# Cross-attention scores in four equal chunks, one per PSUM bank, in a fused decoder layer

## The chip, the cores and the metric

The kernel runs on one core of one Trainium2 chip. The metric is the device time of one execution in microseconds, median of the runs shown. The profile is of one execution on the same core.

## What is computed

One pre-norm decoder layer in fp32 on x of 2048 x 256: page-causal self-attention with rotary embedding (16 heads of 16), then cross-attention to 1601 context rows with one head of width 1024, then a feed-forward layer with quantized activations and ternary weights. The part that the change touches is the cross-attention:

```python
Q = q @ Wq.T + bq
K = k @ Wk.T + bk
V = v @ Wv.T + bv
e = jnp.einsum('bsd,btd->bst', Q, K) / jnp.sqrt(jnp.float32(d_k))
e = jnp.where(mask == 0, MASK_FILL, e)
a = jax.nn.softmax(e, axis=-1)
y = jnp.einsum('bst,btd->bsd', a, V)
return y @ Wo.T + bo
```

Here q is the normed x (2048 x 256), k and v are the context (1601 x 256), and the mask is int32, 2048 x 1601.

## The kernel before

Three stages run one after the other, each a block in which every engine has its own instruction stream and waits on semaphores.

`self_attention` works through 4 blocks of 512 queries. `fold` adds the attention's output to x, norms it, and folds the projections: Wq with Wk into `w_qk` (256 x 256), Wv with Wo into `w_vo`, so that keys and values of width 1024 are never made. It splits the transposed context into a high and a low fp32r piece (`ctx_parts`) and computes the first four of the seven value jobs (a job is two tiles of 128 context rows, V_EARLY = 4 at line 58). The other three stand at the head of the next stage (line 1586).

`cross` is the stage of the change. It walks over 16 tiles of 128 queries. `pairs` writes out tiles 0 and 1, loops over tiles 2 to 13 two at a time, and writes out tiles 14 and 15. The slot h is the tile's parity: the score rows `e[:, h, :]` and the mask rows `mask[:, h, :]` have two slots. For each tile:

- TensorE, `score` (line 1489 on): scores of a tile as products of split fp32r pieces. For each chunk of columns there are six products (two halves of the 256 inner values, three pairs of pieces). The chunks are 512, 512, 512 and 66 columns wide; they fill banks 0 to 3 without gaps, so that the 1601 scores lie in one run. Part 0 is the first two chunks, 12 products; part 1 the other two, 12 products.
- GpSimd, `fill` (line 1295): writes the row's fill value to `e` ahead of the scores. `lower_query` (line 1287) makes the low piece of the query two tiles ahead.
- VectorE, `take`: copies the scores over the fill where the mask is set (line 1323, a predicated copy out of PSUM), takes the maximum (line 1325) and scales it (line 1327).
- ScalarE, `exponential` (line 1452): the exponential in place with the row sum.
- TensorE, `turn_probs` (line 1547): 13 transposes of the exponentials into three banks in four groups, 4 + 4 + 4 + 1. ScalarE copies each group to the high piece (line 1462), VectorE subtracts to get the low piece (line 1378).
- TensorE, value products (line 1577): 13 pairs of 512 and 256 columns into `y_bank`. VectorE scales and adds the result to x (lines 1397 and 1400) and takes the statistics (1404, 1409); GpSimd and VectorE norm the row.

The order is written out by hand. In the body of tile i TensorE does: part 0 of the scores of tile i+1, then (once tile i's exponential is done) 12 transposes of tile i, then part 1 of the scores of tile i+1, the thirteenth transpose, and the 26 value products:

```python
def body(i, h, last):
    if not last:
        score(i + 1, 1 - h, 0)
    ...
    pe.wait_ge(exp_done, i + 1)
    ...
    for n in range(3):
        turn_probs(n)
    if not last:
        score(i + 1, 1 - h, 1)
    pe.wait_ge(p_low, i * NCH + 1)
    turn_probs(3)
```

VectorE in the same body: four subtractions of tile i, `take` of tile i+1, then norm work of earlier tiles and the output of tile i. GpSimd fills `e` for tile i+2 once all 13 transposes of tile i are done. Behind tile 15 come the feed-forward products (lines 1523 and 1534).

Of the kernel before, what the change touches and what calls it, by code (L numbers as in the profile page):

```python
# [18 lines left out]
I32 = mybir.dt.int32  # L19
U32 = mybir.dt.uint32  # L20
ALU = mybir.AluOpType
ACT = mybir.ActivationFunctionType
AX_X = mybir.AxisListType.X
ReduceOp = bass.bass_isa.ReduceOp

P = 128
# [5 lines left out]
BLK = 512  # L32
# [18 lines left out]
S2 = 1601  # L51
S2_TILES = -(-S2 // P)
S2_TAIL = S2 - (S2_TILES - 1) * P
S2_EVEN = S2 + S2 % 2
DH = 1024
HC = DH // P
X_SCALE = float(DH) ** -0.5
# [13 lines left out]
def banks(psum, first, n=1):  # L71
    return psum[:, first * BLK:(first + n) * BLK]
# [717 lines left out]
def fold(nc, ctx, io, keep, psum):  # L790
# [7 lines left out]
    def sem(name):  # L798
        return ctx.enter_context(nc.semaphore(name))
# [5 lines left out]
    qc_parts, qc_high, qc_low = keep["qc_parts"], keep["qc_high"], keep["qc_low"]  # L805
# [58 lines left out]
    ctx_pad = sem("ctx_pad")  # L864
# [9 lines left out]
    with nc.Block() as block:  # L874

        @block.sync
        def _(sp):
            sp.dma_start(b_o[:, :], bass.AP(io["bo"].tensor, 0, [[0, P], [1, E]])).then_inc(b_o_loaded, 16)
            sp.dma_start(ffn_w[:, :, :], io["ffn_w"].rearrange("(c p) e -> p c e", p=P)).then_inc(ffn_w_loaded, 16)
            masks = io["mask"].rearrange("(t p) s -> t p s", p=P)  # L880
            for name in ("gamma", "beta"):
                sp.dma_start(keep[name + "_row"][:, :], bass.AP(io[name].tensor, 0, [[0, P], [1, E]]))\
                    .then_inc(keep["rows_loaded"], 16)
            for h in range(2):
                sp.dma_start(keep["mask"][:, h, :], masks[h]).then_inc(keep["mask_loaded"][h], 16)

        @block.gpsimd
        def _(pool):
            nc.gpsimd.memset(eps[:, :], LN_EPS).then_inc(set_done, 1)  # L889
            nc.gpsimd.memset(minus_half[:, :], -0.5).then_inc(set_done, 1)  # L890
            nc.gpsimd.memset(ones[:, :], 1.0).then_inc(ones_set, 1)
            for part in ctx_parts:
                nc.gpsimd.memset(part[:, :, S2:S2_EVEN].bitcast(F32), 0.0).then_inc(ctx_pad, 1)
            pool.wait_ge(set_done, 2)

            def norm(tb):
                pool.wait_ge(mv_done, tb * TPB + TPB)
                nc.gpsimd.tensor_tensor(var[:, :], mv[:, :, 1], eps[:, :], ALU.add).then_inc(var_done, 1)
                pool.wait_ge(var_done, tb + 1)
                nc.gpsimd.tensor_tensor(rstd[:, :], var[:, :], minus_half[:, :], ALU.pow).then_inc(rstd_done, 1)  # L900

                pool.wait_ge(row_done, 2)
                pool.wait_ge(xn_ready, tb * TPB + TPB)
                tiles = x[:, bass.ds(tb * TPB, TPB), :]
                bias = row_b[:, :].unsqueeze(1).to_broadcast([P, TPB, E])
                nc.gpsimd.tensor_tensor(tiles, tiles, bias, ALU.add).then_inc(bias_added, 1)

            with pool.Fori(0, NB) as tb:
                norm(tb)
            for h in range(2):  # L910
                pool.wait_ge(qc_high, h + 1)
                nc.gpsimd.tensor_tensor(qc_parts[1][:, h, :, :], x2_t[:, :, 0, h * P:(h + 1) * P],
                                        qc_parts[0][:, h, :, :].bitcast(F32), ALU.subtract).then_inc(qc_low, 1)
# [225 lines left out]
def cross(nc, ctx, io, keep, psum):  # L1139
    def sb(name, shape, dt=F32):  # L1140
        return ctx.enter_context(nc.sbuf_tensor(name, shape, dt))

    def sem(name):
        return ctx.enter_context(nc.semaphore(name))
# [7 lines left out]
    x3_low = [flat[tb // 3][:, tb % 3 * EC * BLK:(tb % 3 + 1) * EC * BLK].rearrange("p (c t) -> p c t", c=EC)  # L1152
              for tb in range(NB)]
    mask, w_vo = keep["mask"], keep["w_vo"]
    zeros = sb("zeros_s2", [P, S2])
    qc_parts, qc_high, qc_low = keep["qc_parts"], keep["qc_high"], keep["qc_low"]
    e = sb("e", [P, 2, S2])
    neg = sb("neg", [P, 2])
    esum = sb("esum", [P, 2])
    rsum = sb("rsum_x", [P, 2])  # L1160
# [6 lines left out]
    scale = sb("scale3", [P, 1])  # L1167
# [9 lines left out]

    CHUNKS = [(c * TPB, min(TPB, S2_TILES - c * TPB)) for c in range(-(-S2_TILES // TPB))]
    NCH = len(CHUNKS)
    e_bank = psum[:, 0:S2_EVEN]  # L1180
    t_bank = [banks(psum, n) for n in (4, 5, 7)]
    y_bank = banks(psum, 6)
    v_bank = {4: banks(psum, 6), 5: banks(psum, 7), 6: banks(psum, 5)}
# [5 lines left out]
    mask_loaded, rows_loaded = keep["mask_loaded"], keep["rows_loaded"]  # L1189
# [4 lines left out]
    e_taken = sem("e_taken")  # L1194
    max_done = sem("max_done")
# [45 lines left out]
    with nc.Block() as block:  # L1241

        @block.sync
        def _(sp):
            masks = io["mask"].rearrange("(t p) s -> t p s", p=P)
            with sp.Fori(0, PAIRS - 1) as k:
                for h in range(2):

                    sp.wait_ge(e_taken, 2 * k + h + 1)
                    sp.dma_start(mask[:, h, :], masks[2 * k + (h + 2)]).then_inc(mask_loaded[h], 16)  # L1250

            out = io["out"].rearrange("(u t p) e -> u p t e", p=P, t=2)
            for u in range(UNITS):
                sp.wait_ge(out_added, u + 1)
                sp.dma_start(out[u], x[:, 2 * u:2 * u + 2, :]).then_inc(out_sent, 16)
            sp.wait_ge(out_sent, 16 * UNITS)

        @block.gpsimd
        def _(pool):
# [30 lines left out]
            def fill(i, h):  # L1290
                if isinstance(i, int):
                    value = row_fill[:, i:i + 1]
                else:
                    value = row_fill[:, bass.ds(i, 1)]
                nc.gpsimd.tensor_tensor(e[:, h, :], zeros[:, :], value.to_broadcast([P, S2]),  # L1295
                                        ALU.add).then_inc(filled, 1)

            def body(i, h, last):
# [16 lines left out]
        def _(dve):  # L1315
            def take(i, h):

                dve.wait_ge(mask_loaded[h], (i - h) * 8 + 16)
                dve.wait_ge(filled, i + 1)
                dve.wait_ge(e_ready, i + 1)  # L1320

                dve.sem_inc(waits_met, 1)
                nc.vector.copy_predicated(e[:, h, :], mask[:, h, :], e_bank[:, 0:S2]).then_inc(e_taken, 1)  # L1323
                dve.wait_ge(e_taken, i + 1)
                nc.vector.tensor_reduce(neg[:, h:h + 1], e[:, h, :], axis=AX_X, op=ALU.max).then_inc(max_done, 1)  # L1325
                dve.wait_ge(max_done, 2 * i + 1)
                nc.vector.tensor_scalar(neg[:, h:h + 1], neg[:, h:h + 1], -X_SCALE, None,  # L1327
                                        ALU.mult).then_inc(max_done, 1)
# [114 lines left out]
        def _(act):  # L1443
# [5 lines left out]

            def exponential(i, h):  # L1450
                act.wait_ge(max_done, 2 * i + 2)
                nc.scalar.activation(e[:, h, :], e[:, h, :], ACT.Exp, scale=X_SCALE, bias=neg[:, h:h + 1],  # L1452
                                     accum_out=esum[:, h:h + 1]).then_inc(exp_done, 1)

            def body(i, h, last):
# [29 lines left out]
            for tb in range(NB):  # L1485
                nc.scalar.activation(over[:, tb, :, :], x3_t[:, tb, :, :], ACT.Relu,
                                     bias=bound[:, 1:2]).then_inc(over_done, 1)

        @block.tensor
        def _(pe):  # L1490
            def score(i, h, part):

                if part == 0:
                    pe.wait_ge(e_taken, i)
                    pe.wait_ge(qc_low, i + 1)
                starts = list(range(0, S2, BLK))
                for c0 in (starts[:2], starts[2:])[part]:
                    c1 = min(c0 + BLK, S2_EVEN)
                    products = [(k, *pieces) for k in range(EC) for pieces in ((0, 0), (0, 1), (1, 0))]
                    for k, left, right in products:  # L1500
                        last = nc.tensor.matmul(e_bank[:, c0:c1], qc_parts[left][:, h, k, :],  # L1501
                                                ctx_parts[right][:, k, c0:c1], start=(k, left, right) == products[0],
                                                stop=(k, left, right) == products[-1])
                if part == 1:
                    last.then_inc(e_ready, 1)
# [77 lines left out]
            for n in range(V_EARLY, len(V_JOBS)):  # L1583
                for m, j in enumerate(V_JOBS[n]):
                    for k in range(EC):
                        last = nc.tensor.matmul(v_bank[n][0:keys_of(j), m * E:(m + 1) * E],  # L1586
                                                ctx_t[:, k, j * P:j * P + keys_of(j)], w_vo[:, k, :],
                                                start=k == 0, stop=k == EC - 1)
# [23 lines left out]
def build(nc, io):  # L1612
    with ExitStack() as outer:
        def sb(name, shape, dt=F32):
            return outer.enter_context(nc.sbuf_tensor(name, shape, dt))

        psum = outer.enter_context(nc.psum_tensor("psum", [P, 8 * BLK], F32))
        keep = {"x": sb("x_sb", [P, TILES, E]), "ident": sb("ident", [P, P])}
        with ExitStack() as own:
            def sbo(name, shape, dt=F32):  # L1620
                return own.enter_context(nc.sbuf_tensor(name, shape, dt))
# [18 lines left out]
            keep["w_qk"] = sbo("w_qk", [P, EC, E])  # L1640
            keep["w_vo"] = sbo("w_vo", [P, EC, E])
            keep["ones"] = sbo("ones", [P, P])
            keep["mask"] = sbo("mask", [P, 2, S2], I32)
            keep["gamma_row"] = sbo("gamma_row", [P, E])
            keep["beta_row"] = sbo("beta_row", [P, E])
            keep["mask_loaded"] = [own.enter_context(nc.semaphore(f"mask_loaded{n}")) for n in range(2)]
# [75 lines left out]
```

## Time and profile before

| | |
|---|---|
| median of 3 runs | 813.98 us (813.0 to 814.86) |
| the profiled execution | 815.49 us |
| its span, first to last instruction | 813.6 us |
| mean granted TensorE clock | 0.962 |
| busy: TensorE products, weight loads | 753.8 us, 394.8 us |
| busy: VectorE, ScalarE, GpSimd | 620.8 us, 427.2 us, 150.2 us |
| cross-attention | from 608 us on |

A busy time is the union of an engine's instructions. TensorE's products overlap their successors, and weight loads overlap products, so the price of one product is the distance from one start to the next and not its own duration. The chain of waits lists, from the last instruction backwards, what released each step, and is shown in order of time.

### The profile page before, as it was taken

What the parts mean: (1) busy time and instruction counts of PE and PEld (TensorE: products, weight loads), DVE (VectorE), ACT (ScalarE), POOL (GpSimd) and SP (SyncE); (2) the same over time, 40 slices, a digit from 0 to 9 for tenths busy, and PEclk for the clock granted to TensorE, in tenths of its full rate; (3) what the DMA queues carried; (4) which work ended last, traced back from release to release, by engine and by line L of the source; (5) the groups of instructions that cost most, each with busy time, mean ns of one, the idle gap of its engine ahead of it and who ended that gap; (6) DMA issues with size and microseconds to landing.
All of it is one profiled execution on the core that took longest, in us unless ns stands there. A gap on an engine that the chain in (4) does not pass through costs nothing. (4 is left out here: it accounts for less than half of the span.)

```text
span 813.6 us, 12188 instructions
## 1 busy us (share of the span) xinstructions
PE 753.8 (93%) x4329; PEld 394.8 (49%) x4329; DVE 620.8 (76%) x1107; ACT 427.2 (53%) x879; POOL 150.2 (18%) x170
## 2 busy tenths in 40 slices
PE   7874897999999999999999997989999999999997
PEld 5431232333223333223333331268658888888886
DVE  4899687888998889999888762037736777787885
ACT  1453263676667776666777875932133333333353
POOL 2555000000000000000000000003314555555520
PEclk9997698899999999999999998999999999999999
DMA  7598341020000000000180000030002122222103
GB/s 211 166 254 257 54 118 40 1 67 27 27 2 2 0 2 1 1 1 1 48 254 2 1 1 2 1 114 1 0 1 78 56 70 81 81 81 81 40 1 104
DMA packets 27152, 47.32 MB, mean 58 GB/s; under 512 B 6112, under 2 KB 23008, under 8 KB 26336
## 3 DMA queue, kind: packets, MB, share of 16 engines
q1 hardware_dynamic: 25184, 43.94, 18.0%
q10 hardware_dynamic: 1920, 2.75, 1.2%
q8 instruction: 29, 0.48, 0.3%
q14 instruction: 19, 0.16, 0.1%
HBM read 38.16 MB, written 8.39 MB: 57 GB/s over the span
## 5 line engine op out<-in xcount | busy, mean ns | idle before, releaser
L495 DVE TENSOR_REDUCE part_max<-psum 128x1 f32<-128x512 f32 (+3 forms) x560 | 341.3, 668 | 54.6 <-PE psum L681 49.5
L600 ACT ACTIVATE probs<-psum 128x512 f32<-128x512 f32 (+3 forms) x640 | 293.7, 539 | 154.9 <-PE psum L706 153.9
L681 PE MATMUL psum<-k_stack,q_stack 96*128 96x512 bf16 (+4 forms) x640 | 214.8, 364 | 18.8 <-DVE psum L481 11.5
L706 PE MATMUL psum<-q_stack,k_stack 98*128 98x512 bf16 (+4 forms) x640 | 202.2, 357 | 13.4 <-DMA q_stack<-shift 11.6
L718 PE MATMUL psum<-probs,v_all 128*17 128x512 f32 (+3 forms) x1280 | 149.1, 538 | 0.3
L681 PEld LDWEIGHTS psum<-k_stack,q_stack 96*128 96x128 bf16 (+1 forms) x640 | 60.1, 99 | 171.6 <-DVE part_max L495 120.9
L706 PEld LDWEIGHTS psum<-q_stack,k_stack 98*128 98x128 bf16 (+1 forms) x640 | 60.9, 99 | 94.4 <-ACT probs L600 39.0
L889 POOL MEMSET eps<- 128x4 f32 x1 | 0.1, 102 | 459.0 <-POOLq L282 459.0
L1501 PE MATMUL psum<-ctx_part,qc_part 128*128 128x512 f32 (+1 forms) x384 | 82.9, 366 | 1.8 <-PEq L874 1.8
L1577 PE MATMUL psum<-v_parts,p_part 128*128 128x512 f32 (+3 forms) x416 | 77.3, 342 | 0.0
L1501 PEld LDWEIGHTS psum<-ctx_part,qc_part 128*128 128x128 f32 x384 | 66.3, 189 | 14.5 <-issue 2.6
L1577 PEld LDWEIGHTS psum<-v_parts,p_part 128*128 128x128 f32 (+1 forms) x416 | 64.0, 188 | 8.7
L1452 ACT ACTIVATE e<-e,neg 128x1601 f32<-128x1601 f32 x16 | 26.2, 1636 | 68.0 <-DVE neg L1327 63.4
L1378 DVE TENSOR_TENSOR p_part<-psum,p_part 128x512 fp32r<-128x512 f32 x64 | 34.7, 585 | 25.7 <-ACT p_part L1462 25.7
L1295 POOL TENSOR_TENSOR e<-zeros_s,row_fill 128x1601 f32<-128x1601 f32 x16 | 45.6, 2853 | 35.8 <-PE psum L1547 35.7
L1462 ACT ACTIVATE p_part<-psum 128x512 fp32r<-128x512 f32 x64 | 29.6, 518 | 37.4 <-PE psum L1547 37.4
L718 PEld LDWEIGHTS psum<-probs,v_all 128*17 128x17 f32 x1280 | 21.4, 95 | 49.4 <-ACT probs L600 36.7
L1323 DVE COPY_PREDICATED e<-mask,psum 128x1601 f32<-128x1601 int32 x16 | 33.1, 2069 | 9.8 <-PE psum L1501 9.1
L518 DVE RECIPROCAL rsum<-psum 128x16 f32<-128x16 f32 x16 | 4.1, 253 | 38.1 <-PE psum L692 37.6
L1325 DVE TENSOR_REDUCE neg<-e 128x1 f32<-128x1601 f32 x16 | 29.1, 1821 | 0.6
L1547 PE MATMUL psum<-ident,e 128*128 128x128 f32 (+1 forms) x208 | 28.5, 275 | 1.0 <-DVE p_part L1378 0.7
L1045 PE MATMUL psum<-q_stack 128*128 128x256 f32 (+2 forms) x128 | 26.3, 357 | 0.0
(145 smaller groups left out, 689.2 us busy)
## 6 DMA issues: line engine op xcount, KB each, us to landing
mask<-in_mask SPq DMA_DIRECT2D x16, 800.5 KB, 4.3
pieces<-k_stack SPq DMA_DIRECT2D x24, 256.0 KB, 4.7
q_stack<-pieces SPq DMA_DIRECT2D x24, 256.0 KB, 4.3
k_stack<-pieces SPq DMA_DIRECT2D x24, 256.0 KB, 4.7
x_sb<-in_x SPq DMA_DIRECT2D x4, 512.0 KB, 9.2
out<-x_sb SPq DMA_DIRECT2D x8, 256.0 KB, 2.2
q_stack<-in_ctxT SPq DMA_DIRECT2D x1, 1601.0 KB, 11.0
probs<-in_cos ACTq DMA_DIRECT2D x4, 256.0 KB
```

What stands on the lines that cost most here:

```text
L495: nc.vector.tensor_reduce(part_max[:, h:h + m, r, c:c + 1], src, axis=AX_X, op=ALU.max).then_inc(m_read, 1)
L600: nc.scalar.activation(probs[:, s % 2, h, col:BLK], s_bank[h][:, col:BLK], ACT.Exp, scale=ATTN_SCALE).then_inc(exp_done, 1)
L681: last = nc.tensor.matmul(out, q_stack[b][0:rows, g * G + h, r * P:(r + 1) * P], k_stack[c][0:rows, g * G + h, 0:keys], start=True, stop=True)
L706: nc.tensor.matmul(s_bank[h][:, col:BLK], k_stack[s // TPB][0:rows, g * G + h, (s % TPB) * P:(s % TPB + 1) * P], q_stack[b][0:rows, g * G ...
L718: last = nc.tensor.matmul(o_bank[32 * h:32 * h + VW, col:BLK], v_all[:, s, g * G + h, :], probs[:, s % 2, h, col:BLK], start=s == 0, stop= ...
L1295: nc.gpsimd.tensor_tensor(e[:, h, :], zeros[:, :], value.to_broadcast([P, S2]), ALU.add).then_inc(filled, 1)
L1323: nc.vector.copy_predicated(e[:, h, :], mask[:, h, :], e_bank[:, 0:S2]).then_inc(e_taken, 1)
L1325: nc.vector.tensor_reduce(neg[:, h:h + 1], e[:, h, :], axis=AX_X, op=ALU.max).then_inc(max_done, 1)
L1378: nc.vector.tensor_tensor(p_parts[1][0:rows, j:j + m, :].rearrange("p j q -> p (j q)"), t_bank[n % 3][0:rows, 0:m * P], p_parts[0][0:rows, ...
L1462: nc.scalar.activation(p_parts[0][0:rows, j:j + m, :].rearrange("p j q -> p (j q)"), t_bank[n % 3][0:rows, 0:m * P], ACT.Copy).then_inc(p_ ...
L1501: last = nc.tensor.matmul(e_bank[:, c0:c1], qc_parts[left][:, h, k, :], ctx_parts[right][:, k, c0:c1], start=(k, left, right) == products[ ...
L1577: mm = nc.tensor.matmul(cols, p_parts[part][0:keys, j, :], values, start=j == 0 and part == 0, stop=end and part == 0)
```

## The change

The scores of a tile are computed in four chunks of 402 columns (1608 in all), each at the start of a bank of its own (0 to 3). Part 0 is chunks 0 and 1, part 1 chunks 2 and 3. The context pieces are padded with zeros from 1601 to 1608 columns. `e`, the mask and the zeros are 1608 wide. The predicated copy reads `[128, 4, 402]` out of the four banks; the pad of the mask is set to 0 once, in the folding stage. The maximum and the exponential take the first 1601 elements, as before. The value jobs stay where they were.

```diff
-S2_EVEN = S2 + S2 % 2
+QUARTER = 402
+S2_EVEN = 4 * QUARTER
...
-                sp.dma_start(keep["mask"][:, h, :], masks[h]).then_inc(keep["mask_loaded"][h], 16)
+                sp.dma_start(keep["mask"][:, h, 0:S2], masks[h]).then_inc(keep["mask_loaded"][h], 16)
...
             for part in ctx_parts:
                 nc.gpsimd.memset(part[:, :, S2:S2_EVEN].bitcast(F32), 0.0).then_inc(ctx_pad, 1)
+            nc.gpsimd.memset(keep["mask"][:, :, S2:S2_EVEN], 0).then_inc(ctx_pad, 1)
...
-    zeros = sb("zeros_s2", [P, S2])
+    zeros = sb("zeros_s2", [P, S2_EVEN])
...
-    e = sb("e", [P, 2, S2])
+    e = sb("e", [P, 2, S2_EVEN])
...
-    e_bank = psum[:, 0:S2_EVEN]
+    e_bank = banks(psum, 0, 4).rearrange("p (n s) -> p n s", n=4)
...
-                nc.gpsimd.tensor_tensor(e[:, h, :], zeros[:, :], value.to_broadcast([P, S2]),
+                nc.gpsimd.tensor_tensor(e[:, h, :], zeros[:, :], value.to_broadcast([P, S2_EVEN]),
...
-                nc.vector.copy_predicated(e[:, h, :], mask[:, h, :], e_bank[:, 0:S2]).then_inc(e_taken, 1)
+                quarters = [row[:, h, :].rearrange("p (n s) -> p n s", n=4) for row in (e, mask)]
+                nc.vector.copy_predicated(*quarters, e_bank[:, :, 0:QUARTER]).then_inc(e_taken, 1)
...
-                nc.vector.tensor_reduce(neg[:, h:h + 1], e[:, h, :], axis=AX_X, op=ALU.max).then_inc(max_done, 1)
+                nc.vector.tensor_reduce(neg[:, h:h + 1], e[:, h, 0:S2], axis=AX_X, op=ALU.max).then_inc(max_done, 1)
...
-                nc.scalar.activation(e[:, h, :], e[:, h, :], ACT.Exp, scale=X_SCALE, bias=neg[:, h:h + 1],
+                nc.scalar.activation(e[:, h, 0:S2], e[:, h, 0:S2], ACT.Exp, scale=X_SCALE, bias=neg[:, h:h + 1],
...
-                starts = list(range(0, S2, BLK))
-                for c0 in (starts[:2], starts[2:])[part]:
-                    c1 = min(c0 + BLK, S2_EVEN)
+                for n in (2 * part, 2 * part + 1):
+                    c0, c1 = n * QUARTER, (n + 1) * QUARTER
...
-                        last = nc.tensor.matmul(e_bank[:, c0:c1], qc_parts[left][:, h, k, :],
+                        last = nc.tensor.matmul(e_bank[:, n, 0:QUARTER], qc_parts[left][:, h, k, :],
...
-            keep["mask"] = sbo("mask", [P, 2, S2], I32)
+            keep["mask"] = sbo("mask", [P, 2, S2_EVEN], I32)
```

On TensorE, in the loop body of the cross-attention (a tile's scores at L1501, its transposes at L1547, the value products at L1577), the order before is:

```order
L1501 MATMUL psum<-ctx_part,qc_part 128x512 [waits qc_low]
L1501 MATMUL psum<-ctx_part,qc_part 128x512 x11
L1547 MATMUL psum<-ident,e 128x128 [waits exp_done3]
L1547 MATMUL psum<-ident,e 128x128 x11
L1501 MATMUL psum<-ctx_part,qc_part 128x512 x6
L1501 MATMUL psum<-ctx_part,qc_part 128x66 x6
L1564 ISA
L1547 MATMUL psum<-ident,e 65x128 [waits p_low]
L1577 MATMUL psum<-v_parts,p_part 128x512 [waits p_low,x_added3]
```

And now, where the same lines are L1503, L1549 and L1579:

```order
L1503 MATMUL psum<-ctx_part,qc_part 128x402 [waits qc_low]
L1503 MATMUL psum<-ctx_part,qc_part 128x402 x11
L1549 MATMUL psum<-ident,e 128x128 [waits exp_done3]
L1549 MATMUL psum<-ident,e 128x128 x11
L1503 MATMUL psum<-ctx_part,qc_part 128x402 x12
L1566 ISA
L1549 MATMUL psum<-ident,e 65x128 [waits p_low]
L1579 MATMUL psum<-v_parts,p_part 128x512 [waits p_low,x_added3]
```

The number of products and their waits stay; the six narrow ones at the end of the second group are gone, and all 24 have one width.

## Rows read from the trace of the kernel before

**Rows 1.** The page, busy time: us, share of the span, instructions.

```profile
PE 753.8 (93%) x4329; PEld 394.8 (49%) x4329; DVE 620.8 (76%) x1107; ACT 427.2 (53%) x879; POOL 150.2 (18%) x170
```

**Rows 2.** Chain of waits, cross-attention, in order of time: start us, us, step.

```profile
608.66 5.01 PE psum L1501 x24
...
620.86 1.31 PE psum L1547 x12
...
661.32 2.79 PE psum L1501 x12
664.10 1.31 PE psum L1547 x12
665.41 1.99 PE psum L1501 x12
667.54 4.59 PE psum L1577 x26
672.13 2.79 PE psum L1501 x12
...
773.55 1.99 PE psum L1501 x12
776.40 2.07 DVE e L1323
...
790.39 4.67 PE psum L1523 x40
...
802.91 5.27 PE psum L1534 x48
```

**Rows 3.** Timeline, tiles 4 and 5: start us, us, instruction, idle before it.

```profile
659.72 0.74 POOL L1287 TENSOR_TENSOR qc_part<-x_t,qc_part 128x256 fp32r<-128x256 f32 x1
660.93 2.74 PEld L1501 LDWEIGHTS psum<-ctx_part,qc_part 128*128 128x128 f32 x12
...
663.11 0.18 ACT L1452 ACTIVATION_READ_ACCUMULATOR e<-e,neg 128x1 f32 x1
...
663.94 1.47 PE L1547 MATMUL psum<-ident,e 128*128 128x128 f32 x12
664.34 0.18 DVE L1409 BATCH_NORM_AGGREGATE mv<-stats 128x2 f32<-128x6 f32 x1 [0.24 <-DVE stats L1404]
...
665.21 1.89 DVE L1378 TENSOR_TENSOR p_part<-psum,p_part 128x512 fp32r<-128x512 f32 x3 [0.69 <-ACT p_part L1462]
...
667.88 0.29 DVE L1378 TENSOR_TENSOR p_part<-psum,p_part 65x128 fp32r<-65x128 f32 x1 [0.79 <-ACT p_part L1462]
668.23 2.06 DVE L1323 COPY_PREDICATED e<-mask,psum 128x1601 f32<-128x1601 int32 x1
```

**Rows 4.** Timeline, the last tile, where TensorE waits for the exponential.

```profile
782.14 0.18 ACT L1452 ACTIVATION_READ_ACCUMULATOR e<-e,neg 128x1 f32 x1
...
782.38 1.53 PE L1547 MATMUL psum<-ident,e 128*128 128x128 f32 x12 [0.37 <-ACT e L1452]
```

**Rows 5.** Timeline, the first tile.

```profile
612.90 2.85 POOL L1295 TENSOR_TENSOR e<-zeros_s,row_fill 128x1601 f32<-128x1601 f32 x1
...
619.91 0.18 ACT L1452 ACTIVATION_READ_ACCUMULATOR e<-e,neg 128x1 f32 x1
```

**Rows 6.** Groups by line and form, 490 to 760 us: busy us, mean ns, idle.

```profile
L1501 PEld LDWEIGHTS psum<-ctx_part,qc_part 128*128 128x128 f32 x344 | 59.5, 189 | 13.3 <-issue 2.6
...
L1323 DVE COPY_PREDICATED e<-mask,psum 128x1601 f32<-128x1601 int32 x14 | 29.0, 2069 | 9.7 <-PE psum L1501 9.1
...
L1325 DVE TENSOR_REDUCE neg<-e 128x1 f32<-128x1601 f32 x14 | 25.5, 1821 | 0.5
L1378 DVE TENSOR_TENSOR p_part<-psum,p_part 128x512 fp32r<-128x512 f32 x39 | 24.5, 684 | 11.9 <-ACT p_part L1462 11.9
...
L1378 DVE TENSOR_TENSOR p_part<-psum,p_part 65x128 fp32r<-65x128 f32 x13 | 3.7, 287 | 10.2 <-ACT p_part L1462 10.2
```

**Rows 7.** Stretches: us, busy per engine (PE, PEld, DVE, ACT, POOL), PEclk, DMA share, GB/s.

```profile
613.00:785.00 172.00, 170.95 (x1002) 148.35 (x1001) 134.46 (x215) 62.72 (x112) 87.13 (x102) 1.00 0.20 67
```

More of the change, by code:

```diff
@@ L1249, in _ @@
                     sp.wait_ge(e_taken, 2 * k + h + 1)
-                    sp.dma_start(mask[:, h, :], masks[2 * k + (h + 2)]).then_inc(mask_loaded[h], 16)
+                    sp.dma_start(mask[:, h, 0:S2], masks[2 * k + (h + 2)]).then_inc(mask_loaded[h], 16)
             out = io["out"].rearrange("(u t p) e -> u p t e", p=P, t=2)
```

## Prediction

> **What bounds the kernel now.** I read the page first. TensorE is busy for 93% of the span, VectorE for 76%, the others for much less [rows 1], so TensorE may be the bound, but a busy share is a mean over three stages, and the change touches one: the cross-attention, from 608 us on. The chain of waits in order of time settles it for that stage. Between the first score products and tile 14 it holds TensorE groups and nothing else, with the same four lengths in each tile: 12 products of scores 2.79 us, 12 transposes of the exponentials 1.31, the other 12 score products 1.99, the value products 4.59 [rows 2]. With 0.13 for the thirteenth transpose this makes the period: 672.13 - 661.32 = 10.81 us, 14 times alike from tile 0 to tile 14 (622.17 to 773.55). Only behind tile 14, where no scores are left to compute, does the chain leave TensorE, for VectorE's predicated copy at 776.40 and what follows it: maximum, exponential, transposes.
>
> So each tile is a ring of two loops. The engine loop is what TensorE must do in a tile. The softmax loop runs through the same transposes: transposes, second score group, last transpose, ScalarE's copy and VectorE's subtraction of that transpose, predicated copy, maximum, exponential, and the next tile's transposes. The timeline of tile 4 tells how far the second is behind the first [rows 3]: the exponential's accumulator is read out at 663.11 + 0.18 = 663.29, and the 12 transposes end at 663.94 + 1.47 = 665.41, that is 2.12 later. Where TensorE really waits for the exponential, in the last tile, the same stretch is 782.32 to 783.91, 1.59 us [rows 4]. The softmax loop has **0.53 us of slack**; it would close at 10.28 us.
>
> **The change, part by part.**
>
> *The products.* Before, a tile takes 18 products of 512 columns and 6 of 66; now 24 of 402. A 512-wide one costs 2.79 / 12 = 0.232 us [rows 2]. The narrow ones: second group and last transpose together are 667.54 - 665.41 = 2.13; less a transpose (1.31 / 12 = 0.11) and six wide ones (1.39) leaves 0.63, or 0.104 each, nearly as much as a 128-column transpose. A 66-column product is paid like one of some 230 columns, and that is what the change removes. The trace has no 402-column product. Its price by the wide ones is 402/512 x 0.232 = 0.182; by the last stage's 256-column products of the same type, 4.67 / 40 = 0.117 [rows 2], it is 402/256 x 0.117 = 0.183. I take 0.183. The lower end is the bf16 products of 256 columns, 5.27 / 48 = 0.110, which give 0.172; the upper end is one whole weight load, 0.189 [rows 6], in case each product waited for its own load (the 256-wide ones do not), say 0.188.
> Then the scores cost 24 x 0.183 = 4.39 where they cost 2.79 + 2.13 - 0.11 = 4.81: **the engine loop falls by 0.41, to 10.40 us**. The granted clock is 1.00 from 613 to 785 us [rows 7], so all of these are prices at 2.4 GHz.
> The Trainium skill, "TensorE: Matmul & The Clock Gate", section "Back-to-back issue gap", gives N/2.4 + 2.5 ns for an isolated product. That is 216 ns for 512 columns where the trace has 232, and it would be 170 ns for 402. By it the sum below would be about 8 us and not 5.5, an estimate from that page's figure. I go by the trace, since it is 7% above that rule at 512 and at 256 columns alike.
>
> *Where they stand.* The 12 of the first group get shorter, 2.79 to 2.20, but the second group, which lies on the softmax loop, had the cheap narrow ones and gets longer: 12 x 0.183 + 0.11 = 2.31 instead of 2.13, **+0.18 on the softmax loop**. Its end is not waited for by the predicated copy itself: that starts at 668.23, behind the last subtraction (667.88 + 0.29), which hangs on the last transpose [rows 3]. So the whole shift of the transpose is passed on.
>
> *The predicated copy* reads four runs of 402 instead of one of 1601: 7 elements more, 2069 ns / 1601 x 7 = 0.01 us [rows 6]. That the three gaps between runs cost nothing I assume (the other value is a rival, below). Maximum and exponential still take 1601 elements. The fill on GpSimd grows by 7 elements (0.01 us); the query piece behind it ends at 660.46, and the next scores' weights are loaded at 660.93 [rows 3], and both hang on the last transpose, so that cover of 0.47 stays. The extra memset and the wider pads stand at the start of the folding stage, where GpSimd idles; the mask's DMA keeps its size and gets a tile to land. I cost these at nothing.
>
> *Sum per tile.* The softmax loop closes at 10.81 - 0.53 + 0.18 + 0.01 = 10.47 us, the engine loop at 10.40. The first is now the later: TensorE is predicted to wait for the exponential in each tile, and **0.34 of the 0.41 us arrive**. VectorE must also be free when the transposes come 0.53 sooner behind the exponential: it ends its statistics at 664.34 + 0.18 = 664.52 and starts the subtractions at 665.21 [rows 3], so 0.16 is left. It just holds.
> *Total.* The end of tile 0's transposes: the 24 products at the head get 4.81 - 4.39 = 0.42 shorter; the chain through mask and exponential moves with them, since the first fill is done when the second starts, at 612.90, and the shortened scores end at about 613.67 - 0.42 = 613.25 [rows 2, 5]; then its slack is used up, which is 0.49: the accumulator's 619.91 + 0.18 to the transposes' 620.86 + 1.31 is 2.08, less 1.59 [rows 2, 4, 5]. That is -0.91. Fourteen periods: -4.76. Tile 14 to 15 was bound by the softmax loop already and gets +0.19. Together **-5.5 us**. The profiled execution took 815.49 us (span 813.6), so it would take 810.0; against the median of 813.98 that is **808.5 us**. At 0.172 per product the same sum gives -1.17 - 14 x 0.48 + 0.05 = -7.8, at 0.188 it gives -0.79 - 14 x 0.28 + 0.25 = -4.5. The slack is read against the last tile, whose code is written out and not in a loop; should 0.16 of it not be there in the loop (my allowance), it is about -3.
>
> **The rivals.**
> *A, the engine stays the bound.* The softmax loop would have to be 0.07 shorter than I read it. For it: the two loops end up that close. Against: the second group's lengthening follows from the prices. Time: -1.0 - 14 x 0.41 + 0.2 = -6.5, 807.5 us.
> *B, a 402-column product costs 0.172 or less*, so that the second group hardly grows: -7.8, 806.2 us. Against: both fp32r rows give 0.182 to 0.183. (The rule of the Trainium skill's page on TensorE, section "Back-to-back issue gap", leads to this case.)
> *C, slower: the gathered PSUM read.* If each of the four runs pays a start of its own, the predicated copy, which is on the loop that now binds, gets longer. A VectorE instruction's fixed part is, from the subtraction's 684 ns at 512 and 287 at 128 elements [rows 6], 287 - 128 x 1.034 = 0.155 us; three more make 0.46. The softmax loop is then 10.93 (+0.12), tile 0 moves by -0.45, tile 15 by +0.65: +1.9, 815.9 us. It decides from 5.5 / 16 = 0.34 us more per copy on. For it: this copy takes 2069 ns where the maximum over as many elements takes 1821 [rows 6], so something in it already costs 0.25 us. Against: nothing shows it to be the bank changes.
>
> **How the numbers follow.** My forecast has a chance of 0.70, A 0.07, B 0.08, C 0.08; 0.07 is left for a part of the gain lost in a place that I don't see. This kernel's measurement can tell about 0.2% (1.6 us) from no change. Forecast, A and B lie beyond it, with some of the rest: faster 0.88, same 0.05, slower 0.07. The forecast's own range, by the two prices, is 806.2 to 809.5; with the case of the smaller slack (811) and the scatter of the runs (0.9 to each side) I give 805.8 to 811.6; C lies outside.
>
> **What would show it.** Right: score products 0.183 apart in both groups; a period near 10.47; the chain of waits passing through the predicated copy, the maximum and the exponential in each tile instead of TensorE alone; a wait of TensorE for the exponential of about 0.1 us per tile; the copy at 2.08. Wrong: a period of 10.40 and a chain of TensorE alone (A), products 0.172 or less apart (B), a copy of over 2.3 us (C), or VectorE's first subtraction starting late behind its statistics.

## The result and the profile after

The changed kernel took 805.03 us (median of 4 runs, 804.85 to 806.43), the kernel before 813.6 us (4 runs) beside it. The ratio is 0.9895, with a 95% interval of 0.988 to 0.9909. The forecast of 808.5 had the direction right and the size too small, and the time lies 0.8 us below the range. The profiled execution of the changed kernel took 805.07 us, its span 803.3 us.

The groups of the page, changed kernel (columns as in [rows 6]):

```profile
L1503 PE MATMUL psum<-ctx_part,qc_part 128*128 128x402 f32 x384 | 77.2, 350 | 1.8 <-PEq L875 1.8
...
L1503 PEld LDWEIGHTS psum<-ctx_part,qc_part 128*128 128x128 f32 x384 | 69.6, 189 | 3.3 <-issue 2.6
...
L1326 DVE COPY_PREDICATED e<-mask,psum 128x1608 f32<-128x1608 int32 x16 | 32.0, 2000 | 9.4 <-PE psum L1503 8.7
```

All 384 score products have 402 columns. The predicated copy takes 2000 ns where it took 2069 [rows 6], with 7 elements more.

The chain of waits of the changed kernel in order of time, to be held against [rows 2]:

```profile
606.16 4.66 PE psum L1503 x24
...
617.35 1.39 PE psum L1549 x12
618.75 2.20 PE psum L1503 x12
...
627.86 1.36 PE psum L1549 x12
...
638.32 1.37 PE psum L1549 x12
...
657.01 2.21 PE psum L1503 x12
659.22 1.31 PE psum L1549 x12
660.53 2.21 PE psum L1503 x12
662.74 0.11 PE psum L1549
662.84 4.59 PE psum L1579 x26
667.44 2.21 PE psum L1503 x12
...
764.70 2.20 PE psum L1503 x12
...
781.62 4.68 PE psum L1525 x40
...
789.49 3.08 PE psum L1525 x24
```

A group of 12 score products is 2.21 us, 0.184 each, in both places. The period in tile 4 is 667.44 - 657.01 = 10.43 us, and from tile 0 (617.35 + 1.39 = 618.74) to tile 14 (764.70) it is 145.96 / 14 = 10.425 on average. The chain still holds TensorE alone up to tile 14, as in [rows 2].

The average hides two kinds of period. The first two, which end with the transposes of tiles 1 and 2, take 10.475 us each (618.74 to 639.69), and the groups of transposes of tiles 0 to 2 are longer than the 1.31 us of transposes that wait for nothing. The other twelve take 10.42 (639.69 to 764.70), with 1.31 in each. Before, all fourteen were 10.81. Experiment 3 comes back to this.

The timeline says that this is a near tie. Changed kernel, tile 4 (compare [rows 3]):

```profile
658.74 0.18 ACT L1455 ACTIVATION_READ_ACCUMULATOR e<-e,neg 128x1 f32 x1
...
658.98 1.31 PEld L1549 LDWEIGHTS psum<-ident,e 128*128 128x128 f32 x12
659.05 1.48 PE L1549 MATMUL psum<-ident,e 128*128 128x128 f32 x12
659.30 0.43 DVE L1407 BATCH_NORM_STATS2 stats<-x_sb 128x6 f32 x1
...
662.57 0.27 PE L1549 MATMUL psum<-ident,e 128*65 128x128 f32 x1
...
663.19 0.29 DVE L1381 TENSOR_TENSOR p_part<-psum,p_part 65x128 fp32r<-65x128 f32 x1 [0.81 <-ACT p_part L1465]
663.53 2.01 DVE L1326 COPY_PREDICATED e<-mask,psum 128x1608 f32<-128x1608 int32 x1
```

The transposes' first weights are loaded 0.06 us behind the read-out of the accumulator (658.92 to 658.98), so the exponential does hold them now. They end at 660.53, 1.61 us behind the read-out; the closed loop of the last tile takes 1.59 [rows 4], and before there were 2.12 [rows 3]. The slack is used up. But the last product of the scores still runs, until 659.22 (656.85 + 2.37), when the transposes start at 659.05, and their group in the chain is the shortest, 1.31, so next to nothing is lost by it in this tile.

Where the two profiles differ, stretch by stretch, from the first and last rows of each:

| stretch | before | after | difference | predicted |
|---|---|---|---|---|
| start to the first score product | 608.66 | 606.16 | -2.50 | 0 |
| to the end of tile 0's transposes | 13.51 | 12.58 | -0.93 | -0.91 |
| 14 periods | 151.38 | 145.96 | -5.42 | -4.76 |
| tile 14's to tile 15's transposes | 10.36 | 10.46 | +0.10 | +0.19 |
| behind them to the end | 29.7 | 28.1 | -1.6 | 0 |

The stage of the change gives 6.25 us. The other 4.1 us stand in code that is the same in both kernels, but for one small memset and the wider pads. In both places TensorE's clock differs. Granted clock and busy times of the kernel before, around its last 24 high and low products (columns as in [rows 7]):

```profile
795.00:798.20 3.20, 1.61 (x12) 1.20 (x11) 2.10 (x7) 2.00 (x4) 0.00 (x0) 1.00 0.00 0
798.20:801.70 3.50, 3.43 (x16) 3.43 (x17) 2.04 (x4) 3.41 (x5) 0.00 (x0) 0.52 0.00 0
```

And of the changed kernel in the same place of the program:

```profile
786.30:789.40 3.10, 1.56 (x12) 1.20 (x11) 2.02 (x7) 1.98 (x4) 0.00 (x0) 1.00 0.00 0
...
790.00:793.00 3.00, 3.00 (x28) 2.90 (x28) 1.61 (x3) 3.00 (x4) 0.00 (x0) 1.00 0.02 5
```

TensorE was half idle ahead of both (busy for 1.61 of 3.20 us and 1.56 of 3.10). In the one the clock then stood at 0.52, nearly all of it at the lower level of 1.2 GHz, and the 24 products took 4.64 us; in the other it stayed at 2.4 GHz and they took 3.08. Near the start of the program, between 14 and 20 us, the clock differs too (kernel before, then changed):

```profile
14.00:20.00 6.00, 3.34 (x4) 1.50 (x5) 2.08 (x10) 2.37 (x3) 1.33 (x2) 0.72 0.54 160
```

```profile
14.00:20.00 6.00, 4.37 (x11) 2.01 (x12) 2.54 (x10) 1.47 (x3) 1.33 (x2) 1.00 0.54 154
```

Not all of the 2.50 us of the first row is the clock's. The timelines of the two show that TensorE starts the first eight products of line 639 (in the changed kernel 640) at 16.66 and at 15.63 us, 1.03 apart. They wait for a copy by ScalarE, which is still issuing the loading transfers until 14.10 and 13.07. The eight products then take 5.37 us at the low clock and 3.67 at the full one.

### The profile page after: what moved, and what is told of

The parts are those of the page before. It is cut to its first block and busy times, and to the rows that moved or that the text cites. A ratio compares the mean times of both kernels' runs of the same rounds, so it can differ in the third digit from the quotient of the medians.

```text
span 803.3 us, 12189 instructions
## 1 busy us (share of the span) xinstructions
PE 745.3 (93%) x4329; PEld 397.5 (49%) x4329; DVE 619.4 (77%) x1107; ACT 427.0 (53%) x879; POOL 150.2 (19%) x171
## 5 line engine op out<-in xcount | busy, mean ns | idle before, releaser
L1503 PE MATMUL psum<-ctx_part,qc_part 128*128 128x402 f32 x384 | 77.2, 350 | 1.8 <-PEq L875 1.8
L1579 PE MATMUL psum<-v_parts,p_part 128*128 128x512 f32 (+3 forms) x416 | 77.3, 342 | 0.0
L1503 PEld LDWEIGHTS psum<-ctx_part,qc_part 128*128 128x128 f32 x384 | 69.6, 189 | 3.3 <-issue 2.6
L1579 PEld LDWEIGHTS psum<-v_parts,p_part 128*128 128x128 f32 (+1 forms) x416 | 63.8, 188 | 9.5
L1297 POOL TENSOR_TENSOR e<-zeros_s,row_fill 128x1608 f32<-128x1608 f32 x16 | 45.8, 2866 | 30.9 <-PE psum L1549 30.9
L1465 ACT ACTIVATE p_part<-psum 128x512 fp32r<-128x512 f32 x64 | 29.6, 517 | 32.6 <-PE psum L1549 32.6
L1326 DVE COPY_PREDICATED e<-mask,psum 128x1608 f32<-128x1608 int32 x16 | 32.0, 2000 | 9.4 <-PE psum L1503 8.7
L1549 PE MATMUL psum<-ident,e 128*128 128x128 f32 (+1 forms) x208 | 28.2, 274 | 1.0 <-DVE p_part L1381 0.7
```

Source lines behind the costliest of these rows:

```text
L1326: nc.vector.copy_predicated(*quarters, e_bank[:, :, 0:QUARTER]).then_inc(e_taken, 1)
L1465: nc.scalar.activation(p_parts[0][0:rows, j:j + m, :].rearrange("p j q -> p (j q)"), t_bank[n % 3][0:rows, 0:m * P], ACT.Copy).then_inc(p_ ...
L1503: last = nc.tensor.matmul(e_bank[:, n, 0:QUARTER], qc_parts[left][:, h, k, :], ctx_parts[right][:, k, c0:c1], start=(k, left, right) == pr ...
L1549: last_t = nc.tensor.transpose(t_bank[n % 3][0:keys, (j - j0) * P:(j - j0 + 1) * P], e[:, h, j * P:j * P + keys], ident[:, :])
L1579: mm = nc.tensor.matmul(cols, p_parts[part][0:keys, j, :], values, start=j == 0 and part == 0, stop=end and part == 0)
```

## Experiments

Two things had to be found out: which of the two loops binds before and after, and whether the head and the tail belong to the change.

**1. Is the softmax loop really 10.28 us before, and closed after?** The same small load was put on it in both kernels: a second copy of the first 402 elements.

```diff
+                nc.vector.copy_predicated(e[:, h, 0:402], mask[:, h, 0:402], e_bank[:, 0:402]).then_inc(copied, 1)
+                dve.wait_ge(copied, i + 1)
...
                 nc.vector.copy_predicated(e[:, h, :], mask[:, h, :], e_bank[:, 0:S2]).then_inc(e_taken, 1)
```

Expected of the kernel before with it:

> The kernel before with a second predicated copy of the first 402 elements put ahead of the whole one (same values, about 0.65 us more on the softmax loop with its wait). Theory of the prediction (0.53 us of slack in the softmax loop before): the period grows by only 0.1 to 0.2, from 10.81 to 10.9 or 11.0, and the time by 2 to 4 us. Rival (no slack, or VectorE bound by its own work): the period grows by the whole 0.65, the time by 10 us.

Expected of the changed kernel with it (the copy there is of the first run of 402):

> The changed kernel with the same extra copy of 402 elements. If the softmax loop touches the engine loop after the change, the whole 0.65 us arrives: period 10.42 to about 11.05, time 805 to about 815 us. If it had slack left, less arrives, by the slack.

Measured: the kernel before went to 817.13 us, ratio 1.004 (1.0025 to 1.0054), and its period from 10.813 to 11.076 (mean of 14), so 0.26 of it arrived. The changed kernel went to 819.34 us, ratio to the kernel before 1.0074 (1.005 to 1.0097), its period from 10.425 to 11.192, so 0.77 arrived. The load itself was larger than the 0.65 expected, so both periods lie above what was expected of them (10.9 to 11.0, and 11.05), and the changed kernel's time lies 4 us above the 815. The chain of waits of the changed kernel with the extra copy shows what the prediction had wanted to see without it:

```profile
658.50 0.63 DVE e L1327
...
659.27 2.03 DVE e L1330
661.32 1.83 DVE neg L1332
...
665.14 1.53 PE psum L1553 x12
666.67 2.20 PE psum L1507 x12
```

The extra copy takes 0.62 us in both kernels, so the softmax loop had 0.5 us more slack before. Over the twelve later periods alone the two are at 11.04 and 11.15. With the softmax loop of the changed kernel at 10.38 there (experiment 3), the load costs 11.15 - 10.38 = 0.77, and the loop of the kernel before is 11.04 - 0.77 = 10.27, where the prediction read 10.28 from one tile's timeline.

**2. Out of the way, and deeper in.** One line sets how many chunks of scores lie on the softmax loop.

```diff
-                for n in (2 * part, 2 * part + 1):
+                for n in ((0, 1, 2), (3,))[part]:
```

> The changed kernel with three of the four 402-column chunks in part 0 (ahead of the transposes) and one in part 1 (behind them). TensorE's work per tile is the same; the softmax loop gets 6 products, 6 x 0.184 = 1.10 us, shorter. Theory 1 (the changed kernel is bound by TensorE's own loop, 10.42 us, with the softmax loop only touching it): the period stays 10.40 to 10.43, the exponential's read-out lies a microsecond ahead of the transposes, time within 0.3% of the changed kernel (805 us). Theory 2 (the changed kernel is still bound by the softmax loop): the period falls to the engine loop of the prediction, 10.36 to 10.40, and the time by 0.3 to 1 us more.

Measured: 806.75 us (6 runs), ratio to the kernel before 0.9918 (0.9899 to 0.9937); period 10.413. This is theory 1, in the period and in the time (0.2% above 805). The read-out now lies well ahead of the transposes, as expected:

```profile
658.64 0.18 ACT L1455 ACTIVATION_READ_ACCUMULATOR e<-e,neg 128x1 f32 x1
660.05 1.47 PE L1549 MATMUL psum<-ident,e 128*128 128x128 f32 x12
```

TensorE's own loop is thus 10.41 us, the same in all periods, the first two included. The changed kernel's twelve later periods, 10.42, are within 0.01 of it, and its first two, 10.475, lie 0.06 above. The other direction, `((0,), (1, 2, 3))[part]`:

> The changed kernel with one chunk of scores ahead of the transposes and three behind them, so six more products, 1.10 us, lie on the softmax loop. As that loop touches TensorE's own, the period should grow by the whole 1.10, from 10.42 to 11.5, the time by about 14 x 1.10 = 15 us less what the head gains. If products behind the transposes were not on the path, the period would stay at 10.42.

Measured, in a single run: 822.74 us, period 11.482, so 1.06 of the 1.10 us arrived, as expected. What stands behind the transposes is on the path once the slack is gone, and the two loops are within 0.04 us of each other.

**3. Which one binds?** Shifting the tiles after `zeros_s2` by 32 bytes makes the value products a little cheaper (experiment 5), on TensorE's loop only.

```diff
+    spacer = sb("spacer", [P, 8])
     e = sb("e", [P, 2, S2_EVEN])
```

> The changed kernel with 32 unused bytes ahead of e, so that e and the transposed exponentials start 32 bytes further on. That made the value products 4.53 us per tile instead of 4.59 in the kernel before, on TensorE's loop alone; it should leave the softmax loop as it is. If the changed kernel is bound by TensorE's loop, its period falls by about 0.05, to 10.37; if by the softmax loop (the prediction's view), it stays within 0.02 of 10.42, with the wait after the read-out 0.05 as before. Time: within 0.1% of the changed kernel, or 0.7 us less.

> The same 32 bytes in the kernel with three chunks ahead of the transposes, where the softmax loop has 1 us of slack. Only TensorE's loop can bind here, so the period should fall by the 0.05 of the value products, from 10.41 to 10.36, and the time by about 0.8 us below the changed kernel's: the fastest of the family, if the address does what it did before.

Measured: the first 806.69 us (4 runs), ratio 0.9916 (0.9891 to 0.9941), period 10.394; the second 805.56 us (4 runs), ratio 0.9897 (0.9874 to 0.992), period 10.341. The chains of the first and the second:

```profile
667.16 2.21 PE psum L1504 x12
669.37 1.34 PE psum L1550 x12
670.72 2.21 PE psum L1504 x12
672.92 0.11 PE psum L1550
673.03 4.51 PE psum L1580 x26
```

```profile
669.35 3.30 PE psum L1504 x18
672.65 1.31 PE psum L1550 x12
673.96 1.10 PE psum L1504 x6
675.06 0.11 PE psum L1550
675.17 4.51 PE psum L1580 x26
```

With the softmax loop out of the way, TensorE's loop falls by the whole 0.07, to 10.34. With it in place the fall stops earlier, and the transposes' group shows the wait, 1.34 where it is 1.31: the twelve later periods are 10.38 (the 10.394 is the mean with the first two). So there the softmax loop of the changed kernel is 10.38 us and TensorE's is 10.41: **in twelve of fourteen periods the change is bound by TensorE's loop, by 0.03 us**. The expectation for a softmax bound, within 0.02 of 10.42, was missed by 0.01 and that for a TensorE bound, 10.37, by 0.02, because each loop takes over in the middle.

The first two periods are another matter. They are 10.47 to 10.48 in the changed kernel, in both of its repeats, with the shift and with `odd_rows` (experiment 4), and 10.41 only in `split31`, where the softmax loop is out of the way. There the softmax loop binds, at 10.475. The timelines show why it is longer: in tiles 1 and 2 of both kernels the exponential starts 0.24 to 0.25 us behind the start of the scaling of the maximum (line 1330, changed kernel: 636.14 to 636.39 in tile 2), from tile 3 to 14 it is 0.18 to 0.19 (657.02 to 657.20 in tile 4). In the kernel before, the slack in tiles 1 and 2 was accordingly 0.45 and not 0.53: the read-out ends at 641.75 and the transposes at 643.79 in tile 2, 2.04 apart. These exponentials stand in the bodies that are written out, the faster ones in the loop; what makes the difference was not tested.

**4. Why is the softmax loop 10.38 and not 10.47?** The copy got 0.07 shorter. Two suspects were the reading of four runs and the row start. The kernel before with both `e` and the mask 1608 wide, all else as it was:

> The kernel before with e and the mask 1608 wide, but products, banks and the copy of one run of 1601 as before. It tells what made the predicated copy 2.00 us and not 2.07: the row start (slot 1 then starts on a multiple of 32 bytes), or the reading of four runs of 402 out of four banks. Row start: the copy takes about 2.00 here too. Runs: it stays at 2.07. The period stays 10.81 in both cases, the time 811 to 816 us.

The changed kernel with rows of 1609:

> The changed kernel with the rows of e and mask 1609 wide instead of 1608, so that the second slot starts at an odd multiple of 4 bytes; nothing else differs. If the row layout made the predicated copy 2.00 us, the copy goes back to about 2.07, at least in one slot, and as the softmax loop touches the engine loop, the period grows by 0.03 to 0.08 from 10.42, toward the 10.47 of the prediction. If not, the copy stays at 2.00 and the period at 10.42.

Measured: `pad_only` 813.85 us, ratio 0.9996 (0.9982 to 1.001), period 10.813; `odd_rows` 808.43 us (4 runs), ratio 0.9919 (0.9893 to 0.9945), period 10.404. The copies:

```profile
L1324 DVE COPY_PREDICATED e<-mask,psum 128x1601 f32<-128x1601 int32 x16 | 31.9, 1995 | 9.8 <-PE psum L1502 9.1
```

```profile
L1327 DVE COPY_PREDICATED e<-mask,psum 128x1608 f32<-128x1608 int32 x16 | 31.9, 1993 | 9.4 <-PE psum L1504 8.7
```

The copy is fast with one run, and fast with odd rows: reading four runs costs nothing, and the start of the second row is not it. If the row layout had done it, the odd rows would have put the copy back to 2.07, and they don't. Their period is 0.02 below the 10.42 expected for that case; the value products take 4.56 us there and not 4.59 (more on them at the end). `pad_only` also shows that a faster copy alone is worth nothing before the change, where that loop had slack.

**5. The address.** The kernel before with 32 bytes ahead of `e`, and with rows of 1608 in `e` alone:

> The kernel before with 32 unused bytes per partition ahead of e, so that e starts 32 bytes further on; rows stay 1601 wide. The copy took 2.07 us before, 2.00 with rows of 1608, 1608 in the change and 1609. If the start address of e decides it, the copy takes 2.00 here; if the row pitch of e or the mask decides it, it stays at 2.07. Period 10.81 either way.

> The kernel before with rows of 1608 in e alone; e starts at the same address, the mask keeps its pitch of 1601. If the pitch of e decides it, the copy takes 2.00; if the start address or the mask's pitch does, it stays at 2.07.

Measured, in a single run each: 810.52 and 811.32 us, period 10.767 in both, a thing not expected. With the shift the copy takes 1998 ns on average, as the start address would have it. With the wide rows of `e` neither expectation holds alone, it depends on the slot. Two successive tiles of that kernel's timeline, slot 1 and slot 0:

```profile
644.71 2.01 DVE L1323 COPY_PREDICATED e<-mask,psum 128x1601 f32<-128x1601 int32 x1
...
655.49 2.08 DVE L1323 COPY_PREDICATED e<-mask,psum 128x1601 f32<-128x1601 int32 x1
```

By the addresses of the built programs, `e` and the mask lie 70656 bytes apart (a multiple of 256) in both slots of the kernel before and in slot 0 of `e_rows`, and these are the slow copies. The fast ones have 70684 bytes (slot 1 of `e_rows`), 70688 (`pad_only`, `shift_e`), 70752 (changed) and 70784 (`odd_rows` and the two shifted kernels of experiment 3). So it is not the pitch; where the two tensors lie with respect to each other fits all cases, but nothing was tried that tells it from other rules on addresses.

**6. Head and tail.** The same two programs again.

> The changed kernel once more, beside the kernel before. The stage of the change is 6.3 us shorter in the two profiles (first scores to the last tile's transposes), the medians are 8.6 us apart. In the profiles seen so far the stretch ahead of the first scores takes 606.3 or 608.6 us and the stretch behind the last transposes 28.1 or 29.7 us, by whether TensorE's clock stood at its lower level in it, in kernels of both kinds. Theory 1 (these two are chance, the change is worth 6.3 us): with more runs the medians come to 6 to 7.5 us apart. Theory 2 (the change also makes the low stretches rarer): they stay 8 to 9 us apart.

> The kernel before, profiled again. Theory 1: head 606 or 608.6 us, tail 28.1 or 29.7 us, in some combination, and the stage itself as in the first profile (period 10.81). Theory 2: head or tail long again, as in its first profile.

> The changed kernel a third time. Theory 1 (worth 6.3 us in its stage, the rest chance of the head and tail): median 806 to 808.5 us, the distance to the kernel before 6 to 7.5 us. Theory 2: 805 us, 8 to 9 us apart.

Measured: the changed kernel 807.0 us (6 runs; ratio 0.991, 0.989 to 0.9929) and 806.06 us (6 runs; 0.9914, 0.9891 to 0.9936), the kernel before 813.74 us (12 runs; 0.9996, 0.9979 to 1.0013). The last 24 products of the changed kernel in `a_again`:

```profile
789.85 4.58 PE psum L1525 x24
```

So this happens to the changed kernel too. The kernel before, in `b_again`, has both a late first score product (607.80) and the slow 24 products (4.63) once more, as theory 2 wanted it, and its stage and period are those of the first profile. The medians are 7.2 us apart in `a_again`, which is theory 1, and 7.9 in `a_third`, between the two theories, though its 806.06 lies in the range of theory 1.

Over all profiles of this study, six of kernels with the old chunks and nine with the new ones, the first score product starts at 607.4 and 607.5 us on average (606.0 to 608.7 and 606.1 to 610.4), and the tail is long (29.6 to 29.7 and not 28.1 to 28.2) in two of six and four of nine. The head is late with a low clock between 14 and 20 us, in three of six and five of nine, and at 606.0 to 606.9 in all the others. Nothing in these profiles ties head or tail to the chunks. All 16 runs of the changed kernel have a mean of 806.3 us and a median of 806.3, the 74 of the kernel before 813.8 and 814.0: 7.5 us, with a standard deviation of 1.2 and 1.4 us, so about 0.7 to either side. Without the first four runs it is 7.2. The first comparison had drawn the changed kernel's lucky end. Theory 1 had said 6 to 7.5, and theory 2 8 to 9. The 1 us between 7.2 or 7.5 and the 6.25 of the stage I cannot place. No stretch of the profiles shows it, and it is a little more than the 0.7 allows for, so it stays open.

## Why the prediction was right or wrong

- *The products.* 0.183 us predicted, 0.184 measured (2.21 / 12). Right. The 256-column products behind that price lie outside [rows 7], but the clock was 1.00 from 789 to 795 us as well. The formula for an isolated product in the Trainium skill, "TensorE: Matmul & The Clock Gate", section "Back-to-back issue gap", N/2.4 + 2.5 ns, makes it 170 ns; the trace has 8% more, about as at 512 columns.
- *TensorE's loop.* 10.40 predicted, 10.41 measured where it stands alone (`split31`). Right.
- *Slack before, 0.53, and the softmax loop at 10.28.* Confirmed for the loop's tiles: a load that cost 0.77 after cost 0.26 before. The slack was read in tile 4; in tiles 1 and 2 it is 0.45 (experiment 3), which the prediction did not look at. The +0.18 of the second group was right too: from the end of the 12 transposes to the start of the predicated copy it was 668.23 - 665.41 = 2.82 us and is now 663.53 - 660.53 = 3.00.
- *Tile 0.* -0.91 predicted, -0.93 measured.
- *"7 elements more, 0.01 us" for the predicated copy*: **this step failed.** Its price moved by -0.07, not by +0.01, and it is the term that decided between the two loops: in the twelve later periods the softmax loop is 10.38 and not 10.47, TensorE's at 10.41 binds, and the mean period is 10.425. Rival A is what happened there, and the 0.07 by which its softmax loop had to be shorter is about what the copy gave (0.39 of a saving of 0.40 arrived, and not 0.34). The rival had 0.07 of the chance. The term is worth 14 x 0.045 + 0.09 = 0.7 us. I had treated a copy's price as a function of its length alone. In the first two periods TensorE does wait for the exponential and the period is the forecast's 10.47, but by luck: the copy is 0.07 shorter there too, and the slack was 0.08 smaller than read.
- *The total.* Stage: -6.25, predicted -5.5. Rival C was wrong: four runs read as fast as one. VectorE was not late where it counts: in every second tile its first subtraction waits 0.31 to 0.33 us for ScalarE's first copy, in the others it starts right behind the statistics (670.52 + 0.18, then 670.75 in tile 5), so the predicted 0.16 is used up there; but the first three subtractions end at 672.64, a microsecond before the fourth starts at 673.61.
- *The range, and head and tail at nothing*: **this step failed too, and it is the larger part.** Of the 3.5 us between 808.5 and 805.03 the stage has 0.75 (6.25 less 5.5); the other 2.7 lie in stages that the change leaves alone, with the 1 us that stays open. I took the scatter from three runs, 0.9 us to either side, and gave even less of it: 806.2 - 0.9 is 805.3, where I wrote 805.8. Over 74 runs the kernel before lies between 810.7 and 818.5 us. What varies in the profiles is a low stretch of the clock at the head and one at the tail, which come or stay away; the two extreme runs were not profiled. [Rows 7] were read for the stage alone, and the other stages were costed at nothing without asking how they vary. A profiled execution at 815.49 with a median of 813.98 was a sign of that. With 2 us of scatter on the lower side the range would have held the time. The 806.3 of all 16 runs does lie in it.

The fastest version of the family is `split31_shift`, three chunks ahead of the transposes and 32 bytes ahead of `e`: from the first score product to tile 15's transposes it takes 167.7 us, the changed kernel 169.0 and the kernel before 175.25. Its four runs have a median of 805.56 us; by runs alone the 1.3 us can't be told from the changed kernel's 806.3.

## What to carry to other kernels

A 66-column product cost 0.104 us here, nearly what one of 256 columns costs (0.117), so four equal chunks beat three full ones with a remainder. Here each chunk had a bank of its own; no other placing was tried. Where a loop of one engine and a dependency loop share instructions, write down the length of both and count what the edit adds to each. Once they lie within 0.1 us of each other the forecast must be given for both outcomes, since any term of that size decides. And before a difference of 1% is read, see how far the same program scatters and in which stretches.

## What the runs showed of the hardware

- Score products with fp32r operands, one start to the next at 2.4 GHz: 0.232 us at 512 columns, 0.184 at 402, 0.104 at 66. 256 columns take 0.117.
- The predicated copy of 1601 elements takes 2.07 or 2.00 us with the same instruction. Where `e` and the mask lie with respect to each other fits all cases, other rules on addresses were not excluded. Four runs in four banks cost it nothing.
- Value products, 26 per tile: they depend on where the transposed exponentials start, whose slices are their weights (their other operand lies at one address in all these kernels). By the addresses of the built programs, and counted from the kernel before (4.59 us): 64 and 128 bytes further on (`pad_only`, changed) it is 4.58 to 4.60, at 32 (`shift_e`, `e_rows`) and 160 (experiment 3) 4.51 to 4.53, at 192 (`odd_rows`) 4.55 to 4.56. That is the 0.05 to 0.07 of the periods 10.767 and 10.341, found while looking for something else. The high and the low piece moved together, so which of the two does it wasn't separated.
- From the read-out of the accumulator on ScalarE to the weight load that waits for it on TensorE it is 0.05 us in all waiting tiles.
- From the scaling of the maximum on VectorE to the exponential on ScalarE, start to start: 0.24 to 0.25 us in tiles 1, 2 and 15, whose exponentials stand in the bodies that are written out, 0.18 to 0.19 in tiles 3 to 14, in both kernels.
- The clock's low stretches are not the same in each execution of one program. The one in the tail costs 1.5 us (24 products in 4.64 or 3.08).
